# ScalarE's W1/W3 work in an attention and FFN block: scaling and rounding by halves, squares in step 11, sums by twos, and V's bound one group later

## The chip, the cores and the metric

One core of a Trainium2 chip runs the whole kernel in one launch. The metric is the device time in microseconds. Three runs of the kernel before gave 975.13, 976.01 and 978.0 us; the median is 976.01 us.

## What is computed

```python
xn = layernorm(x)                         # x: 2 x 1024 x 512
q, k, v = xn @ Wq.T, xn @ Wk.T, xn @ Wv.T # 16 heads of 32
scores = q @ k.T / sqrt(32), causal
s = (softmax(scores) @ v) @ Wo.T
hidden = silu(xn @ W1.T) * (xn @ W3.T)    # 2048 wide
hidden = fwht(hidden)                     # Walsh-Hadamard, / sqrt(2048)
g = silu(hidden @ W2.T)
return x + s * g
```

Inputs and output are fp32.

## The kernel before

Two batches of 1024 rows are worked off one after the other, each in three stages: project (Q, K, V and the first heads' maxima), heads (16 heads of attention, and beside head j the FFN's hidden tile j of W1 and W3), and tail (output projection, the down projection, the gate). Exactness is kept by splitting each operand into a rounded high part and a low rest, so most products are three matmuls. The transform is applied to W2 instead of hidden: GpSimd does butterfly steps on four slabs of W2 (slab_step), TensorE the last 128-point part in batch 0's tail.

**Heads.** A head has twelve steps (NS = 12, steps 0 to 11), each a tile of transposed scores: widths 512, 384, 256, 128, then 512 five times, 384, 256, 128. The five engines run program orders written out by hand, indexed by the global step g = 12 j + s. In step s of head j:

- TensorE makes scores(g) (line 1455), which needs exp(g - 2) to be done since there are two score banks; a share of the 48 FFN matmuls of tile j (FFN_SHARE, line 1494); maxima of later heads (line 1439); the context of four steps at a time, in steps 7, 10 and 3 of the next head; and in step 7 the transpose of the next head's maxima (line 1445). FFN groups alternate between two banks. The second bank is free again when VectorE's hide (line 1190) is done; it runs in steps 4 and 11.
- ScalarE does exp(g) (line 819), then probs_hi(g - 1) (line 829, the rounding to fp16), in some steps tanh, copies of the context, and the W1/W3 work below.
- GpSimd masks diagonal tiles (line 656, steps 0 to 3 and 8 to 11), combines the context, forms the low parts of W1/W3 in four pieces after exps 3 to 6 of the head (line 664), and in batch 0 does butterfly steps: in heads 0 to 2 some of slab 2, in heads 4 to 11 two of slab 3, after the masks of steps 10 and 11.
- VectorE does maxima (line 1148), probs_lo(g - 1) (line 1161, subtracts p_hi), gate, hide, and m_lo.
- SP's queue issues, per head, the three loads of the stack for head j + 2, in batch 0 the scan load of tile j + 4, the load of W1/W3 tile j + 2 (waits for GpSimd's last low piece), and the two stores of the maxima. After head 3's it stores slab 2 and loads slab 3.

**W1/W3.** A tile is 128 x 2 x 512 in fp32 (W1 part, W3 part). It is scaled by a power of two per tile (scale_w13, line 811, in place, two 128x512 instructions) and rounded to fp16 (w13_high, line 864, one 128x1024 instruction). The power comes from the mean square of the tile over all rows: in batch 0 a second load of each tile (scan) is squared and summed along its rows by ScalarE (w13_squares, line 854), TensorE adds over partitions (sum_of_squares, line 1421) and VectorE makes the scales of a group of tiles with five small operations (scale_of_w13). Tile 0 is its own group, tiles 1 to 3 are the second, then come groups of SCAN_GROUP tiles. There is one buffer for scans from tile 4 on, so the scan load of tile t waits for the squares of tile t - 1.

**V's bound.** In batch 0's project stage TensorE multiplies ones with the absolute values of Wv after projection group BOUND_AFTER (bound_of_v, line 1408). It waits for x16_lo of tile 6 (and so for all before it) because its bank M held the transposes. VectorE turns the result into a scale, scales Wv in place (line 1012) after the groups in WV_AT, ScalarE rounds (line 736) one group later, VectorE subtracts (line 1016) two groups later. The first V group (group 16) needs all of it. SP's scans of tiles 2 and 3 load into wv_raw and wait for the same.

Of the kernel before, what the change touches and what calls it, by code (L numbers as in the profile page):

```python
# [29 lines left out]
P = 128  # L30
# [37 lines left out]
SQUARES_AT, W13_AT = 5, 2  # L68
WO_AT = [1, 2, 7, 9]
WV_ABS_AFTER = {5: (0, 1), 6: (2, 3)}  # L70
BOUND_AFTER = 8
WV_AT = {9: (0, 1), 10: (2, 3)}
# [14 lines left out]
SCAN_FIRST, SCAN_GROUP = 4, 3  # L87
# [22 lines left out]
def build(nc, x, wq, wk, wv, wo, w1w3, w2, hadamard, out):  # L110
# [6 lines left out]
    with ctx:  # L117
# [15 lines left out]
        with ExitStack() as r:  # L133
# [9 lines left out]
        w13_ssq = sb("w13_ssq", [P, JT], F32)  # L143
        w13_pow, w13_scale, w13_half, w13_unscale = (
            sb(n, [P, JT], F32) for n in ("w13_pow", "w13_scale", "w13_half", "w13_unscale"))
# [17 lines left out]
        with ExitStack() as r:  # L163
# [14 lines left out]
            sb("room_before_x", [P, 2 * D - 2 * NT - 3 * P - W], F32, r)  # L178
# [145 lines left out]
        SUM_PLAN = {scan_groups[n][-1] - SCAN_FIRST: n for n in range(1, len(scan_groups))}  # L324
# [280 lines left out]
        def _(pool):  # L605
# [53 lines left out]
            def w13_low(n, piece):  # L659

                pool.wait_ge(w13_hi_done, n + 1)
                at = (slice(None), piece // 2, slice(piece % 2 * (D // 2), (piece % 2 + 1) * (D // 2)))
                pool.wait_ge(w13_scaled, 2 * n + piece // 2 + 1)
                pool.tensor_tensor(w13_lo[n % 2][at], w13[at], w13_hi[n % 2][at], ALU.subtract  # L664
                                   ).then_inc(w13_lo_done, 1)
# [63 lines left out]
        def _(act):  # L729
# [26 lines left out]
            def project(b):  # L756
# [34 lines left out]
                for t in range(NT):  # L791
# [4 lines left out]
                    if t == 1:  # L796
                        scale_w13(b * NH)
                        w13_high(b * NH)
# [6 lines left out]
            def scale_w13(n):  # L805
# [4 lines left out]
                for m in range(2):  # L810
                    act.activation(w13[:, m, :], w13[:, m, :], ACT.Copy, scale=w13_scale[:, n % NH:n % NH + 1]
                                   ).then_inc(w13_scaled, 1)
# [44 lines left out]
            def w13_high(n):  # L857

                if n < NH:
                    act.wait_ge(w13_scale_step, scale_steps(n))  # L860
                act.wait_ge(w13_in, (n + 1) * 16)
                after(act, ffn_ps, (n - 1) * GROUPS)
                act.wait_ge(w13_scaled, 2 * n + 2)
                act.activation(w13_hi[n % 2][:], w13[:], ACT.Copy).then_inc(w13_hi_done, 1)  # L864
# [8 lines left out]
            def heads(b):  # L873
# [5 lines left out]
                for g in range(SLOTS + DRAIN):  # L879
# [14 lines left out]
                    if s == W13_AT - 1 and j + 1 < NH:  # L894
                        scale_w13(n0 + j + 1)
                    if s == W13_AT and j + 1 < NH:
                        w13_high(n0 + j + 1)
# [745 lines left out]
```

## Time and profile before

| | |
|---|---|
| median of the runs | 976.01 us |
| the profiled execution | 981.31 us |
| its span | 979.6 us |
| mean granted TensorE clock | 0.994 |
| PE busy | 947.8 us (97%) |
| DVE busy | 732.3 us (75%) |
| ACT busy | 619.0 us (63%) |
| POOL busy | 337.8 us (34%) |

PE is TensorE (PEld its weight loads), DVE VectorE, ACT ScalarE, POOL GpSimd, SP SyncE (SPq its DMA queue). Busy time is the union of an engine's instructions; matmuls overlap one another, so a busy PE is not PE at its peak. "Idle before, releaser" is the time in which an engine had nothing to run, and what ended it. The heads of batch 0 begin at about 88 us; those of batch 1 end at about 861 us. The granted clock of a stretch is given as a share of 2.4 GHz.

### The profile page before, as it was taken

Reading aid. Unit: us, or ns where it says so; the run is one execution under the profiler, and the core shown is the slowest. Engines: PE = TensorE matmul, PEld = TensorE weight load, DVE = VectorE, ACT = ScalarE, POOL = GpSimd, SP = SyncE. Lnnn points to the kernel's source line nnn. Section 1 sums busy time; section 2 is a strip of 40 time slices with the busy share of each in tenths; the row PEclk is TensorE's granted clock in tenths of the full one; section 3 lists DMA queues with packets and bytes.
Section 4 is the critical chain, followed back from the end, with each engine's and each line's share of the span. In section 5 each row is a group of like instructions: output and inputs, shape, how many; then the busy total and the mean of one; then the engine's idle time right before and its main releaser. Section 6 shows DMA issues by size and latency. Waiting matters only on the chain. (4 is left out here: it accounts for less than half of the span.)

```text
span 979.6 us, 18781 instructions
## 1 busy us (share of the span) xinstructions
PE 947.8 (97%) x6404; PEld 652.1 (67%) x6404; DVE 732.3 (75%) x1487; ACT 619.0 (63%) x1284; POOL 337.8 (34%) x588
## 2 busy tenths in 40 slices
PE   8899999799999999999999999999999999999997
PEld 7786555455555565788888875565666656578886
DVE  7877998688998988655655568988989898833343
ACT  4445878588888787643344338888788887833221
POOL 1995663355555444000000013534444344410000
PEclk9999999899999999999999999999999999999999
DMA  9695335523433412892116722232322322171111
GB/s 289 235 307 171 87 101 152 128 77 98 129 78 98 110 44 74 280 361 71 44 54 236 230 73 65 77 87 56 99 66 77 88 69 63 45 320 67 43 43 44
DMA packets 57919, 118.46 MB, mean 121 GB/s; under 512 B 5600, under 2 KB 22624, under 8 KB 57312
## 3 DMA queue, kind: packets, MB, share of 16 engines
q1 hardware_dynamic: 57824, 117.27, 39.5%
q8 instruction: 51, 0.84, 0.4%
q14 instruction: 44, 0.36, 0.1%
HBM read 83.43 MB, written 33.55 MB: 119 GB/s over the span
## 5 line engine op out<-in xcount | busy, mean ns | idle before, releaser
L1161 DVE TENSOR_TENSOR p_lo<-stages,p_hi 128x512 f16<-128x512 f32 (+2 forms) x288 | 204.6, 716 | 56.7 <-ACT p_hi L829 52.5
L1494 PE MATMUL f<-x_hi,w_hi 128*128 128x512 f16 x512 | 195.7, 382 | 9.0 <-DVE hidden L1190 9.0
L1494 PE MATMUL f<-x_hi,w_lo 128*128 128x512 f16 x512 | 196.9, 385 | 0.0
L1494 PE MATMUL f<-x_lo,w_hi 128*128 128x512 f16 x512 | 195.6, 382 | 0.0
L819 ACT ACTIVATE stages<-s 128x512 f32<-128x512 f32 (+2 forms) x288 | 150.7, 523 | 53.9 <-PE s L1455 50.4
L829 ACT ACTIVATE p_hi<-stages 128x512 f16<-128x512 f32 (+2 forms) x288 | 159.6, 554 | 27.9 <-POOL stages L656 12.4
L1455 PE MATMUL s<-qk_st 98*128 98x512 f32 (+2 forms) x384 | 166.2, 434 | 6.3 <-ACT stages L819 6.3
L1148 DVE CUSTOM_DVE_ANT_0 m<-m,causal 128x1024 f32<-128x1024 f32 (+3 forms) x128 | 131.1, 1024 | 2.4 <-PE m L1439 2.3
L656 POOL TENSOR_SCALAR_AFFINE_SELECT stages<-stages 128x128 f32<-128x128 f32 x192 | 59.8, 319 | 188.8 <-ACT stages L819 188.7
L664 POOL TENSOR_TENSOR w_lo<-w,w_hi 128x256 f16<-128x256 f32 x128 | 96.0, 777 | 65.4 <-ACT w_hi L864 53.7
L1228 DVE TENSOR_TENSOR h_lo<-hidden,h_hi 128x1024 fp32r<-128x1024 f32 x32 | 39.2, 1225 | 84.6 <-ACT h_hi L914 84.6
L914 ACT ACTIVATE h_hi<-hidden 128x1024 fp32r<-128x1024 f32 x32 | 34.0, 1061 | 105.4 <-PE f L1305 105.4
L1303 PE MATMUL f<-g_hi,h_hi 128*128 128x512 f32 x256 | 99.7, 389 | 0.0
L1304 PE MATMUL f<-g_lo,h_hi 128*128 128x512 f32 x256 | 99.6, 389 | 0.0
L1305 PE MATMUL f<-g_hi,h_lo 128*128 128x512 f32 x256 | 99.6, 389 | 0.0
L1494 PEld LDWEIGHTS f<-x_hi,w_lo 128*128 128x128 f16 x512 | 50.2, 98 | 63.7 <-issue 32.8
L1439 PE MATMUL m<-qk_st 96*128 96x512 f32 (+3 forms) x256 | 91.8, 440 | 0.6 <-DVE mx L1148 0.6
L1455 PEld LDWEIGHTS s<-qk_st 98*128 98x128 f32 x384 | 73.2, 191 | 22.4 <-ACT stages L819 7.6
L1494 PEld LDWEIGHTS f<-x_lo,w_hi 128*128 128x128 f16 x512 | 50.5, 99 | 53.3 <-issue 8.7
L1473 PE MATMUL o<-vparts,p_hi 128*128 128x65 f16 x1152 | 83.7, 194 | 1.0 <-DVE p_lo L1161 1.0
L1494 PEld LDWEIGHTS f<-x_hi,w_hi 128*128 128x128 f16 x512 | 50.9, 99 | 50.3 <-issue 18.0
L1475 PE MATMUL o<-vparts,p_lo 128*128 128x65 f16 x1152 | 83.1, 193 | 0.0
(200 smaller groups left out, 1960.3 us busy)
## 6 DMA issues: line engine op xcount, KB each, us to landing
qk_st<-qk_parts SPq DMA_DIRECT2D x96, 256.0 KB, 4.3
w<-w1w SPq DMA_DIRECT2D x32, 512.0 KB, 3.6
qk_parts<-qk_hi SPq DMA_DIRECT2D x32, 256.0 KB, 3.4
qk_parts<-qk_lo SPq DMA_DIRECT2D x32, 256.0 KB, 4.3
scan<-w1w SPq DMA_DIRECT2D x12, 512.0 KB, 5.8
wht_in<-w SPq DMA_DIRECT2D x4, 1024.0 KB, 11.0
w_butterflied<-wht_in SPq DMA_DIRECT2D x4, 1024.0 KB, 5.9
w_transformed<-g_hi SPq DMA_DIRECT2D x8, 512.0 KB, 3.1
```

Of the source, the lines that this page charges most:

```text
L664: pool.tensor_tensor(w13_lo[n % 2][at], w13[at], w13_hi[n % 2][at], ALU.subtract).then_inc(w13_lo_done, 1)
L819: act.activation(expd[q % NE][:, 0:end - need], SB[q % 2][:, 0, need - start:end - start], ACT.Exp).then_inc(exp_done, 1)
L829: act.activation(p_hi[s][:], expd[q % NE][:, 0:end - need], ACT.Copy).then_inc(p_hi_done, 1)
L1148: dve.tensor_tensor_reduce(out=bank, in0=bank, in1=causal[:, S - width:S], scale=1.0, scalar=LOWEST, op0=ALU.add, op1=ALU.max, accum_out=m ...
L1161: dve.tensor_tensor(p_lo[s][:], expd[q % NE][:, 0:end - need], p_hi[s][:], ALU.subtract).then_inc(p_lo_done, 1)
L1303: pe.matmul(o, a_hi, b_hi, start=first, stop=False)
L1304: pe.matmul(o, a_hi, b_lo, start=False, stop=False)
L1305: return pe.matmul(o, a_lo, b_hi, start=False, stop=last)
L1439: mm = pe.matmul(bank[:, at:end], q[0:STACK, t * P:(t + 1) * P], k[0:STACK, at:end], start=True, stop=True)
L1455: pe.matmul(SB[q % 2][:, 0, 0:end - start], k_st[n % NH % 3][0:STACK + 2, k * P:(k + 1) * P], q_st[n % NH % 3][0:STACK + 2, start:end], st ...
L1473: pe.matmul(o, p_hi[s][:, at:at + P], v, start=k == 0 and t == c * TPC, stop=False, skip_group_check=True)
L1494: mm = pe.matmul(F[m][:, 0, :], w, v, start=k == 0, stop=k == GMM - 1)
```

## The change

- The squares of tiles 4 to 15 move from step 5 of heads 0 to 11 to step 11.
- Scale and round work by halves: the W1 half is scaled in step 1, rounded in step 2; the W3 half is scaled in step 2, rounded in step 3. In the project stage both halves are scaled and then both rounded. GpSimd's low pieces wait for their own half.
- Groups of tiles from tile 4 on have two tiles (six groups where there were four), and a group's sum is taken in step 7 of the head after the one that squared its last tile.
- V's bound and everything on Wv come one group later (in both batches for the scaling and the splits).
- w13_ssq and w13_pow (16 values a partition each) lie in a region that is reused later.

```diff
--- before.py
+++ after.py
@@ -65,11 +65,12 @@
 LOWEST = -3e38
 CTX_AT = [7, 10, 15]
 COPY_AT = [8, 4]
-SQUARES_AT, W13_AT = 5, 2
+SQUARES_AT = 11
+SCALE_AT, HIGH_AT = [1, 2], [2, 3]
 WO_AT = [1, 2, 7, 9]
 WV_ABS_AFTER = {5: (0, 1), 6: (2, 3)}
-BOUND_AFTER = 8
-WV_AT = {9: (0, 1), 10: (2, 3)}
+BOUND_AFTER = 9
+WV_AT = {10: (0, 1), 11: (2, 3)}
 MAX_BEFORE = {1: [0], 2: [1, 2], 3: [3, 4], 4: [5, 6], 5: [7]}
 MT_BEFORE = 7
 NB = 4
@@ -84,7 +85,7 @@
 SCAN_AFTER = {10: (1,), 13: (2, 3)}
 SQUARES_AFTER = {8: (0,), 13: (1,)}
 SQUARES_OF_V = {4: (2,), 5: (3,)}
-SCAN_FIRST, SCAN_GROUP = 4, 3
+SCAN_FIRST, SCAN_GROUP = 4, 2
 SPLIT_WK_AFTER, ROOT_AFTER = 1, 2
 BUSY_FIRST, BUSY_LAST = 42, 6
 STATS_AT = [(0, 1), (1, 1)]
@@ -140,9 +141,7 @@
         stats = sb("stats", [P, NT, 6], F32)
         mv = sb("mv", [P, NT, 2], F32)
         var, std, rstd, tmp = (sb(n, [P, NT], F32) for n in ("var", "std", "rstd", "tmp"))
-        w13_ssq = sb("w13_ssq", [P, JT], F32)
-        w13_pow, w13_scale, w13_half, w13_unscale = (
-            sb(n, [P, JT], F32) for n in ("w13_pow", "w13_scale", "w13_half", "w13_unscale"))
+        w13_scale, w13_half, w13_unscale = (sb(n, [P, JT], F32) for n in ("w13_scale", "w13_half", "w13_unscale"))
 
 
         with ExitStack() as r:
@@ -175,7 +174,8 @@
             m_lo = sb("m_lo", [NT, P], F32R, r)
             ones_r = sb("ones_r", [P, P], F32R, r)
             qk_lo3 = sb("qk_lo3", [P, W], F32R, r)
-            sb("room_before_x", [P, 2 * D - 2 * NT - 3 * P - W], F32, r)
+            w13_ssq, w13_pow = (sb(n, [P, JT], F32, r) for n in ("w13_ssq", "w13_pow"))
+            sb("room_before_x", [P, 2 * D - 2 * NT - 3 * P - W - 2 * JT], F32, r)
             x16_hi = sb("x16_hi", [P, KT, S], F16, r)
             x16_lo = sb("x16_lo", [P, KT, S], F16, r)
             vparts = sb("vparts", [P, NT, NH, VC], F16, r)
@@ -321,7 +321,7 @@
             return X[:, 0, W - len(scan_groups[n]):W]
 
         scan_groups = [range(1), range(1, SCAN_FIRST)] + [range(t, t + SCAN_GROUP) for t in range(SCAN_FIRST, NH, SCAN_GROUP)]
-        SUM_PLAN = {scan_groups[n][-1] - SCAN_FIRST: n for n in range(1, len(scan_groups))}
+        SUM_PLAN = {-1: 1, **{scan_groups[n][-1] - SCAN_FIRST + 1: n for n in range(2, len(scan_groups))}}
 
         def scan_tile(t):
 
@@ -658,7 +658,7 @@
 
             def w13_low(n, piece):
 
-                pool.wait_ge(w13_hi_done, n + 1)
+                pool.wait_ge(w13_hi_done, 2 * n + piece // 2 + 1)
                 at = (slice(None), piece // 2, slice(piece % 2 * (D // 2), (piece % 2 + 1) * (D // 2)))
                 pool.wait_ge(w13_scaled, 2 * n + piece // 2 + 1)
                 pool.tensor_tensor(w13_lo[n % 2][at], w13[at], w13_hi[n % 2][at], ALU.subtract
@@ -794,22 +794,23 @@
                     act.activation(vparts[:, t, :, 0:DH], group_bank(g).rearrange("p (h d) -> p h d", h=NH),
                                    ACT.Copy).then_inc(proj_hi_done, 1)
                     if t == 1:
-                        scale_w13(b * NH)
-                        w13_high(b * NH)
+                        for m in range(2):
+                            scale_w13(b * NH, m)
+                        for m in range(2):
+                            w13_high(b * NH, m)
                     if b == 0:
                         for tile in SQUARES_OF_V.get(t, ()):
                             w13_squares(tile)
                     if t == MT_BEFORE - 1:
                         maxima_hi(b * NH)
 
-            def scale_w13(n):
+            def scale_w13(n, m):
 
                 act.wait_ge(w13_in, (n + 1) * 16)
                 if n < NH:
                     act.wait_ge(w13_scale_step, scale_steps(n))
-                for m in range(2):
-                    act.activation(w13[:, m, :], w13[:, m, :], ACT.Copy, scale=w13_scale[:, n % NH:n % NH + 1]
-                                   ).then_inc(w13_scaled, 1)
+                act.activation(w13[:, m, :], w13[:, m, :], ACT.Copy, scale=w13_scale[:, n % NH:n % NH + 1]
+                               ).then_inc(w13_scaled, 1)
 
             def exp(q):
                 c, k = STEPS[q % NS]
@@ -854,14 +855,11 @@
                 act.activation(scan_tile(n) if n else w13_hi[0][:], scan_tile(n), ACT.Square,
                                accum_out=w13_ssq[:, n:n + 1]).then_inc(w13_sum, 1)
 
-            def w13_high(n):
-
-                if n < NH:
-                    act.wait_ge(w13_scale_step, scale_steps(n))
-                act.wait_ge(w13_in, (n + 1) * 16)
+            def w13_high(n, m):
+
                 after(act, ffn_ps, (n - 1) * GROUPS)
-                act.wait_ge(w13_scaled, 2 * n + 2)
-                act.activation(w13_hi[n % 2][:], w13[:], ACT.Copy).then_inc(w13_hi_done, 1)
+                act.wait_ge(w13_scaled, 2 * n + m + 1)
+                act.activation(w13_hi[n % 2][:, m, :], w13[:, m, :], ACT.Copy).then_inc(w13_hi_done, 1)
 
             def maxima_hi(n):
                 act.wait_ge(mt_ps, n + 1)
@@ -891,10 +889,11 @@
                             tanh(n0 + jf, c)
                     if b == 0 and s == SQUARES_AT and j + SCAN_FIRST < NH:
                         w13_squares(j + SCAN_FIRST)
-                    if s == W13_AT - 1 and j + 1 < NH:
-                        scale_w13(n0 + j + 1)
-                    if s == W13_AT and j + 1 < NH:
-                        w13_high(n0 + j + 1)
+                    for m in range(2):
+                        if s == SCALE_AT[m] and j + 1 < NH:
+                            scale_w13(n0 + j + 1, m)
+                        if s == HIGH_AT[m] and j + 1 < NH:
+                            w13_high(n0 + j + 1, m)
                     if g - 1 in MT_PLAN:
                         maxima_hi(n0 + MT_PLAN[g - 1])
                     if 0 <= g - SLOTS - CT_AT - 1 < 2:
```

## Rows read from the trace of the kernel before

**Rows 1.** Waits of PE: us in total, times, longest us.

```profile
PE f L1494 <- DVE hidden L1190: 9.0, 10, 1.0
PE s L1455 <- ACT stages L819: 6.3, 1, 6.3
...
PE m L1408 <- DVE x_lo L1059: 1.3, 1, 1.3
```

**Rows 2.** Line 1445, five stretches: ns min/median/max, first to last start (us).

```profile
L1445 PE MATMUL xs<-ident,mx x4: 272/273/275, 101.5 to 157.7; 128*8 128x128 f32 x4
...
L1445 PE MATMUL xs<-ident,mx x2: 272/273/274, 157.7 to 175.2; 128*8 128x128 f32 x2
...
L1445 PE MATMUL xs<-ident,mx x2: 273/274/274, 175.2 to 201.5; 128*8 128x128 f32 x2
...
L1445 PE MATMUL xs<-ident,mx x8: 272/272/276, 201.5 to 332.4; 128*8 128x128 f32 x8
...
L1445 PE MATMUL xs<-ident,mx x15: 272/273/274, 597.6 to 840.0; 128*8 128x128 f32 x15
```

**Rows 3.** Head 4: ACT timeline; window 181:186, its last three PEclk, DMA, GB/s.

```profile
180.24 1.06 ACT L854 ACTIVATE scan<-scan 128x1024 f32<-128x1024 f32 x1 [7.33 <-DMA scan<-w1w]
...
181.00:186.00 5.00, 4.08 (x10) 1.89 (x11) 2.75 (x4) 5.00 (x13) 1.39 (x3) 0.50 0.32 105
```

**Rows 4.** SP's queue, 166 to 172: issues, then (last number) us to landing.

```profile
166.47 4.64 SPq L377 DMA_DIRECT2D qk_st<-qk_parts  x3
171.16 0.42 SPq L497 DMA_DIRECT2D scan<-w1w  x1
...
qk_st<-qk_parts SPq DMA_DIRECT2D x2, 256.0 KB, 6.9
scan<-w1w SPq DMA_DIRECT2D x1, 512.0 KB, 9.1
```

**Rows 5.** ACT in head 5: the squares and the exp behind them.

```profile
199.12 1.05 ACT L854 ACTIVATE scan<-scan 128x1024 f32<-128x1024 f32 x1
...
200.16 0.59 ACT L819 ACTIVATE stages<-s 128x512 f32<-128x512 f32 x1
```

**Rows 6.** A head of batch 1: ACT and DVE, steps 11 to 0.

```profile
672.39 0.41 ACT L829 ACTIVATE p_hi<-stages 128x256 f16<-128x256 f32 x1
673.69 0.60 ACT L819 ACTIVATE stages<-s 128x512 f32<-128x512 f32 x1 [0.89 <-PE s L1455]
...
672.83 0.42 DVE L1161 TENSOR_TENSOR p_lo<-stages,p_hi 128x256 f16<-128x256 f32 x1 [0.37 <-ACT p_hi L829]
```

**Rows 7.** Head 6, end: timeline of POOL, DVE and PE.

```profile
227.13 1.27 POOL L642 TENSOR_TENSOR wht_in<-wht_in 128x512 f32<-128x512 f32 x1
...
227.14 1.55 DVE L1161 TENSOR_TENSOR p_lo<-stages,p_hi 128x256 f16<-128x256 f32 x1
228.61 0.73 DVE L1190 SCALAR_TENSOR_TENSOR hidden<-hidden,w_unscale,f 128x512 f32<-128x512 f32 x1
...
229.40 0.39 PE L1494 MATMUL f<-x_hi,w_hi 128*128 128x512 f16 x1 [1.02 <-DVE hidden L1190]
```

**Rows 8.** Head 4, end: timeline of DVE and POOL.

```profile
190.15 0.42 DVE L1161 TENSOR_TENSOR p_lo<-stages,p_hi 128x256 f16<-128x256 f32 x1 [0.21 <-ACT p_hi L829]
...
190.24 1.47 POOL L642 TENSOR_TENSOR wht_in<-wht_in 128x512 f32<-128x512 f32 x1
```

**Rows 9.** Groups by line: xcount | busy us, mean ns | idle before.

```profile
L1421 PE MATMUL xs<-w_ssq,ones_r 128*128 128x3 f32 (+1 forms) x12 | 1.7, 210 | 0.0
```

**Rows 10.** ACT's groups by line and form, the same columns.

```profile
L829 ACT ACTIVATE p_hi<-stages 128x512 f16<-128x512 f32 x160 | 99.5, 622 | 0.2
...
L864 ACT ACTIVATE w_hi<-w 128x1024 f16<-128x1024 f32 x32 | 33.8, 1057 | 0.2
```

**Rows 11.** Project stage of batch 0: timeline of DVE and PE.

```profile
58.39 2.94 DVE L1016 TENSOR_TENSOR w_lo<-wv_raw,w_hi 128x512 fp32r<-128x512 f32 x2
...
63.03 0.39 PE L1303 MATMUL f<-w_hi,xt_hi 128*128 128x512 f32 x1
```

## The prediction

> **What bounds the kernel.** I read the waits of TensorE first, then the spacing of heads, then the places where the spacing breaks. The waits name three things [rows 1]: ten waits of up to 1.0 us on VectorE's line 1190, one of 6.3 us on an exp of ScalarE, one of 1.3 us on VectorE's line 1059. They add up to less than what is lost, because matmuls overlap and a short stop hides in them. So I take one TensorE instruction that comes once a head, the transpose of the maxima in step 7, and measure from one to the next. In batch 1 it is (840.0 - 597.6) / 14 = 17.31 us a head [rows 2]. In batch 0 the three heads up to 157.7 and the seven from 201.5 to 332.4 take 18.7 us each, head 3 to 4 takes 17.5, head 4 to 5 takes 26.3. The work on TensorE is the same in both batches except for the small sums of squares. From 101.5 to 332.4 batch 0 spends 230.9 us on twelve heads; at batch 1's pace it would be 207.8. **23.1 us** is what batch 0 loses in that stretch, and it is where the squares of W1/W3 are.
>
> The 26.3 us head is one event. ScalarE sits for 7.33 us in front of the squares of tile 8, waiting for the tile [rows 3]; all later exps stand behind it in program order, TensorE runs out of scores to make and stops for 6.3 us, and afterwards its granted clock is 0.50 (the 1.2 GHz level) over 181 to 186. Clock and stop together are 26.3 - 17.3 = 9.0 us. The tile was late because the queue of SP had store_slab(2) and load_slab(3), 1 MB each, ahead of it: the next stack's loads took 4.64 us to issue, the scan was issued at 171.16 and landed 9.1 us later, at 180.2 [rows 4].
>
> **The squares, moved to step 11.** In step 5 ScalarE is in its densest stretch: the squares start at 199.12 and the exp behind them at 200.16, so each costs 1.04 us of ScalarE there and everything up to step 10 is 1.04 us late [rows 5]. In step 11 ScalarE has room: in a head of batch 1 it waits 0.89 us for TensorE right behind p_hi of step 10 [rows 6]. 1.04 us put there (they overlap p_hi's end by 0.1) delays one exp by about 0.1 us, and that exp has two slots of TensorE's work before its score bank is wanted, so I cost the squares at nothing in their new place; without that gap it would be 1.04 us a head. The late tile: step 7's transpose of head 4 is at 175.2, step 11's squares come 5.9 us later (ScalarE's p_hi of step 10 starts at 672.39, 5.6 after the transpose of that head at 666.8, and lasts 0.4) [rows 2, 6], at 181.1; the tile lands at 180.2. It just fits, with 0.9 us to spare, and if it slips it meets the idle gap first. What is late next there is stack 6, whose last part is issued at about 170.2 and lands 6.9 later, at 177.1 [rows 4]; TensorE's first maxima of head 6 want it some 2 us after 175.2, so at most some tenths are lost. SP's queue is the other thing that the move touches: the scan of the next tile waits for the squares, which end about when SP has issued the stack; the W1/W3 load behind it waits anyway for GpSimd's last low piece, which comes after step 6's exp of that head. Nothing.
>
> How much of the other 1.4 us a head comes back? Two things are mixed in it. In head 6 line 1190 starts at 228.61 and TensorE gets to go at 229.40 after 1.02 us of idling [rows 7]. Ahead of line 1190 on VectorE stands the p_lo of step 10, and it takes 1.55 us where the same form takes 0.42 in batch 1 [rows 6, 7]: it ends 0.3 us after a butterfly step of GpSimd that started 10 ns before it (227.13 + 1.27). So 1.1 us of lateness is GpSimd's, and step 9's p_lo has a butterfly step beside it too. Heads 0 to 2 and 4 to 11 have these butterfly steps; head 3 has none, pays 17.5 and not 18.7. But head 4, whose ScalarE and VectorE were ahead of the slow TensorE, has them too and loses nothing by them: p_lo of step 10 starts at 190.15, the second butterfly step only at 190.24 [rows 8]. With ScalarE 1.04 us earlier, the masks and with them the butterfly steps start some 0.9 us earlier against TensorE, and TensorE itself is ready some 0.4 us earlier (1.4 lost less 1.0 seen as idle). Then it goes one of two ways: p_lo of step 10 starts first, as in head 4, and line 1190 is in time: 0. Or GpSimd starts first, and 1.0 (seen) + 0.15 (the part of a stop that hides behind the matmul before it) - 0.9 + 0.4 = 0.6 us a head is left. In head 6 the two starts are 10 ns apart [rows 7], so I can't tell which and take the middle, **0.3 us in each of 11 heads, 3.3 us** (0 to 6.6). The squares' term is 23.1 - 3.3 = 19.8 us.
>
> The rule behind this is in the Trainium skill, SBUF — State Buffer, section SBUF: two separate sides: VectorE with two SBUF inputs and GpSimd take a shared port pair as an exclusive lock, whoever starts first, for the whole instruction. The rows agree, and read strictly the rule gives either end, 0 or 6.6 us, not my middle.
>
> **Sums every second head.** Two more sums: twelve records of line 1421 with 1.7 us are six sums, each under 0.3 us of TensorE [rows 9], so 2 x 0.3 = 0.6 us at most; VectorE's five small operations for a sum are in the mean of 18.7 us of batch 0 already, where every third head has them, and VectorE isn't TensorE's releaser there. I take **0.5 us lost** together. The sums are asked for in step 7 and their last squares ended with step 11 of the head before, so TensorE doesn't wait for them.
>
> **Scaling and rounding by halves.** A 128x1024 rounding lasts 1057 ns, a 128x512 one 622 [rows 10], and the next instruction starts about 0.1 us before the end of the last. So two halves cost 2 x 0.52 against 0.96, **0.09 us of ScalarE a head**, 2.8 us over 32 tiles. In batch 1 ScalarE has a gap of 0.89 us a head between steps 11 and 0 alone [rows 6], so TensorE sees nothing; if that cover were gone it would be 2.8 us. The exps of steps 2 and 3 come 0.4 to 0.6 us earlier; nobody waits for them, since heads without squares run at 17.31 with TensorE busy throughout. GpSimd's low pieces wait for step 3's exp and step 4's copy, behind the second half as well. Cost 0, range -0.5 to 2.8. The Trainium skill, ScalarE: Activation LUTs, section What ACT_TABLE_LOAD costs, speaks against halves: 186 ns + 0.833 ns an element, 93 ns of it overlapped, so a split costs 93 ns. The rows give the same, and by that rule all 32 would be 3 us if ScalarE set the pace.
>
> **V's bound one group later.** TensorE idles 1.3 us ahead of it, for VectorE's x16 of tiles 6 and 7 [rows 1]. A group (2.7 us) later these are done: 1.3 us back. But the scale, and all eight operations on V's weights, follow one group later on VectorE, and in batch 0 they take 1.4 us each beside the butterflies (two end at 61.33; V's first group starts at 63.03) [rows 11]. VectorE is back to back from group 9 on; I get its last split at 62.0 us, 0.7 later than now (a group of 2.7 us later, less TensorE's 1.3 and the room of 0.7 between groups), and TensorE there at 63.03 - 1.3 = 61.7. So 1.3 - 0.3 = **1.0 us gained** (0 to 1.3). In batch 1 nothing waits.
>
> **Sum.** 19.8 - 0.5 + 1.0 - 0 = 20.3 us. The profiled execution, 981.3 us (span 979.6), would come to 961.0. The median of the runs is 976.0, 5.3 below it; the stop and the spacing belong to the program, so I take the same off: **955.7 us**. Moving two small tensors of 64 bytes a partition changes no instruction.
>
> **Rivals.**
> (a) GpSimd always starts first, in all 11 heads: 11 x 0.6 = 6.6 us are left in place of 3.3, 959. For it: head 6 [rows 7]. Against it: head 4 [rows 8]. The rule of the Trainium skill's page SBUF — State Buffer named above gives just this if GpSimd wins each time.
> (b) Line 1190 is late because of the butterflies alone and the squares' shift does nothing for it. Then only the hidden 0.4 us a head, head 3's 0.2 and head 4's 8 us come back: 4.0 + 0.2 + 8 + 0.5 = 12.7, 963.3. Against it: head 4 again.
> (c) The stop at head 4 doesn't go but shrinks, because scan or stack 6 lands later than in this trace: 2 to 5 us more, 958 to 961.
> (d) The other side: ScalarE's stretch from step 11 to step 1 of the next head turns critical. The squares hold exps, p_hi and tanh, TensorE waits for the gate, and the whole squares are paid, plus the wait for a tile that is now asked for only after step 11. Against today's loss of 23 us it must cost over 1.9 us in each of 12 heads, that is, the tile must land more than 2 us behind step 11; it is issued some 17 us before and lands in 6 to 9. At 2.2 us a head it would be 979.
> (e) The move does nothing: tiles too late in step 11 also. That is (c) or (d).
>
> **Chances.** The forecast with its middle (952 to 958.9) 0.52; (a) 0.2; (b) 0.13; (c) 0.1; (d) 0.03; the rest is between. Best case: 23.1 - 0.3 + 1.3, 951.9. Down to 951 and up to 964, (a), (b) and (c) are inside. 0.3% (about 3 us) is what a measurement can tell here. Faster by more 0.95, within 0.02, slower 0.03.
>
> **What would show it.** Right: no wait on the scan tile, no 6.3 us stop, no stretch at 0.50 in batch 0's heads; transposes 17.3 to 17.9 us apart in heads 0 to 11; line 1190's waits gone or at 0.6; the wait ahead of line 1408 gone, perhaps a shorter one at V's first group. Wrong: spacing still at 18 us or more, a new wait on stack loads near head 4, or batch 1's spacing off 17.31, which would mean that the halves cost.

## The result and the profile after

The changed kernel takes **964.16 us** (median of four runs, 963.12 to 969.42) against 975.65 us for the kernel before (four runs, 975.13 to 978.0): a ratio of 0.9888, 95% interval 0.9849 to 0.9928. The forecast was 955.7 us with a range of 951 to 964, so the direction was right and the time 8.5 us off, just outside the range. The profiled execution took 964.6 us, 0.4 above its median.

The head of the page after, with the engines' busy times (share of the span, instructions):

```profile
span 962.9 us, 18863 instructions
PE 943.5 (98%) x6408; PEld 651.6 (68%) x6408; DVE 735.5 (76%) x1497; ACT 624.4 (65%) x1316; POOL 335.6 (35%) x588
```

TensorE is still the bound. Its waits after (us in total, times, longest), to be put beside [rows 1]:

```profile
PE f L1493 <- DVE hidden L1189: 5.7, 10, 1.0
...
PE s L1454 <- DMA qk_st<-m_lo: 0.4, 1, 0.4
```

The 6.3 us wait on ScalarE at head 4 and the wait ahead of V's bound are gone. The hide waits went from 9.0 to 5.7 us, which is far from gone, and a small wait on a store of the maxima's rows is new in the list. The same transpose as in [rows 2], after (ns min/median/max, first to last start):

```profile
L1444 PE MATMUL xs<-ident,mx x4: 272/272/273, 100.5 to 155.1; 128*8 128x128 f32 x4
...
L1444 PE MATMUL xs<-ident,mx x2: 273/273/273, 155.1 to 172.5; 128*8 128x128 f32 x2
...
L1444 PE MATMUL xs<-ident,mx x2: 272/272/273, 172.5 to 190.6; 128*8 128x128 f32 x2
...
L1444 PE MATMUL xs<-ident,mx x8: 272/272/275, 190.6 to 316.6; 128*8 128x128 f32 x8
...
L1444 PE MATMUL xs<-ident,mx x15: 272/272/273, 579.5 to 823.2; 128*8 128x128 f32 x15
```

The seven spacings from 190.6 on take 126.0 us, 18.0 each where they took 18.7. Head 3 to 4, which has no butterfly step, takes 17.4; head 4 to 5 takes 18.1 instead of 26.3. Batch 1 has become **slower**: 243.7 / 14 = 17.41 us a head, where [rows 2] give 242.4 / 14 = 17.31.

The span fell by 979.6 - 962.9 = 16.7 us. The transposes cut it into pieces. The first transpose comes at 84.0 instead of 84.9, and 16.5 us instead of 16.6 pass to the second (1.0 us gained). The twelve heads take 216.1 instead of 230.9 (14.8 gained). From 316.6 to batch 1's 579.5 are 262.9 us, from 332.4 to 597.6 they were 265.2 (2.3 gained). Batch 1's fourteen spacings lose 1.3, and behind them nothing changes (139.7 us and 139.6). 1.0 + 14.8 + 2.3 - 1.3 is 16.8, the rest is rounding. But the medians differ by 11.5 us only, so some 5 us of the 16.7 are peculiar to the one execution of the kernel before that was profiled; the experiments show which.

### The profile page after: what moved, and what is told of

The parts are those of the page before. It is cut to its first block and busy times, and to the rows that moved or that the text cites. A ratio compares the mean times of both kernels' runs of the same rounds, so it can differ in the third digit from the quotient of the medians.

```text
span 962.9 us, 18863 instructions
## 1 busy us (share of the span) xinstructions
PE 943.5 (98%) x6408; PEld 651.6 (68%) x6408; DVE 735.5 (76%) x1497; ACT 624.4 (65%) x1316; POOL 335.6 (35%) x588
## 5 line engine op out<-in xcount | busy, mean ns | idle before, releaser
L1160 DVE TENSOR_TENSOR p_lo<-stages,p_hi 128x512 f16<-128x512 f32 (+2 forms) x288 | 211.6, 743 | 33.0 <-ACT p_hi L830 32.7
L1147 DVE CUSTOM_DVE_ANT_0 m<-m,causal 128x1024 f32<-128x1024 f32 (+3 forms) x128 | 131.0, 1023 | 2.3 <-PE m L1438 2.3
L656 POOL TENSOR_SCALAR_AFFINE_SELECT stages<-stages 128x128 f32<-128x128 f32 x192 | 62.2, 330 | 168.7 <-ACT stages L820 168.0
L1472 PEld LDWEIGHTS o<-vparts,p_hi 128*128 128x128 f16 x1152 | 74.1, 97 | 12.8 <-DVE p_lo L1160 1.2
```

The lines of the kernel that those rows point to most:

```text
L1147: dve.tensor_tensor_reduce(out=bank, in0=bank, in1=causal[:, S - width:S], scale=1.0, scalar=LOWEST, op0=ALU.add, op1=ALU.max, accum_out=m ...
L1160: dve.tensor_tensor(p_lo[s][:], expd[q % NE][:, 0:end - need], p_hi[s][:], ALU.subtract).then_inc(p_lo_done, 1)
L1472: pe.matmul(o, p_hi[s][:, at:at + P], v, start=k == 0 and t == c * TPC, stop=False, skip_group_check=True)
```

## Experiments

Twelve kernels were run in three sessions, each with the kernel before beside them (975.53, 975.95 and 976.6 us). Ratios are against those. "Spacing" is the time between two step-7 transposes.

### Is it the halves, the butterflies, or the squares?

**The changed kernel with whole tiles again** (two scalings in step 1, one 128x1024 rounding in step 2, as before):

```diff
-                    for m in range(2):
-                        if s == SCALE_AT[m] and j + 1 < NH:
+                    if s == 1 and j + 1 < NH:
+                        for m in range(2):
                             scale_w13(n0 + j + 1, m)
-                        if s == HIGH_AT[m] and j + 1 < NH:
-                            w13_high(n0 + j + 1, m)
+                    if s == 2 and j + 1 < NH:
+                        w13_high(n0 + j + 1)
```

> The changed kernel with scaling and rounding of a tile whole again (both scalings in step 1, one 128x1024 rounding in step 2). Theory H (the halves cost 0.1 us of ScalarE a head and ScalarE sets the pace of steps 1 to 4): batch 1's spacing falls from 17.41 back to 17.31 us, batch 0's too by 0.1, about 3 us faster than the changed kernel, 961 us. Rival (the 0.1 us a head comes from the shifted addresses or the later work on Wv): spacing stays 17.41, 964 us.

Measured: 961.75 us (961.21 to 965.72), ratio 0.9861 (0.984 to 0.9881), 2.4 us under the changed kernel. Batch 1's transposes in this kernel:

```profile
L1443 PE MATMUL xs<-ident,mx x14: 272/273/273, 598.6 to 824.4; 128*8 128x128 f32 x14
```

225.8 / 13 = 17.37 us; two spacings among them are longer (17.81, which holds a wait of 0.23 us for the store of a maxima row, and 17.63), the eleven others are back at 17.31. The heads with butterflies stay at 17.9 to 18.1. Over all profiles the median spacing of batch 1 is 17.31 us in the eight profiles of kernels that round whole tiles and have batch 1 otherwise unchanged, and 17.40 to 17.41 in the five with halves. So the halves cost 0.10 us in each head that nothing else holds up: batch 1, and in batch 0 heads 3, 12 and 13 (17.41, 17.56, 17.40 with halves; 17.32 in the combined kernel below, 17.47, 17.31 here). In the heads with butterflies they cost nothing, and the first spacing of a batch is 0.15 us shorter with them (16.23 against 16.38 in batch 1). That is about 1.4 us in all; the 2.4 between the medians is within the spread of the runs.

**The changed kernel with one butterfly step of a head moved** from behind step 11's mask to behind step 2's (heads 0 to 2 and 5 to 11), so that none stands beside the p_lo ahead of the hide:

```diff
                         mask(n * NS + s)
+                        if s == 2:
+                            if n < LAST_SLAB_AT - 1:
+                                late_steps(1)
+                            if b == 0 and 0 < j - LAST_SLAB_AT < 8:
+                                of = j - LAST_SLAB_AT
+                                slab_step(D // P - 1, of // 2, of % 2, 0)
...
-                        if n < LAST_SLAB_AT - 1 and s >= NS - 2:
+                        if n < LAST_SLAB_AT - 1 and s == NS - 2:
                             late_steps(1)
                         of = j - LAST_SLAB_AT
-                        if b == 0 and 0 <= of < 8 and s >= NS - 2:
+                        if b == 0 and of == 0 and s >= NS - 2:
                             slab_step(D // P - 1, of // 2, of % 2, s - NS + 2)
+                        if b == 0 and 0 < of < 8 and s == NS - 2:
+                            slab_step(D // P - 1, of // 2, of % 2, 1)
```

> The changed kernel with the butterfly step that followed step 11's mask moved behind step 2's mask of the same head (heads 0 to 2 and 5 to 11); that of step 10 stays. Theory B (the 0.5 to 0.6 us a head left in batch 0 is step 11's butterfly holding the p_lo of step 10, and with it line 1189): waits on line 1189 vanish, spacing of those heads 17.4 to 17.5 us, 5 to 6 us faster, about 958.5 us. Rival (the rest is due to the squares in step 11, on ScalarE): spacing stays near 18.0, 964 us.

Measured: 961.72 us (961.0 to 962.36), 0.9854 (0.9833 to 0.9876), 2.4 us under the changed kernel, where 5.7 were expected. The end of head 6 shows how it works. In the changed kernel (timelines of POOL, DVE and PE: start, us, instruction, idle before; L656 is GpSimd's mask, L642 its butterfly step, L1147 a maximum of VectorE):

```profile
214.57 0.45 POOL L656 TENSOR_SCALAR_AFFINE_SELECT expd<-expd 128x128 f32<-128x128 f32 x1
214.99 1.28 POOL L642 TENSOR_TENSOR wht_in<-wht_in 128x512 f32<-128x512 f32 x1
...
214.12 0.74 DVE L1160 TENSOR_TENSOR p_lo<-stages,p_hi 128x384 f16<-128x384 f32 x1
214.79 0.28 DVE L1147 CUSTOM_DVE_ANT_0 xs<-xs,causal 128x128 f32<-128x128 f32 x1
...
215.00 1.55 DVE L1160 TENSOR_TENSOR p_lo<-stages,p_hi 128x256 f16<-128x256 f32 x1
...
216.47 0.73 DVE L1189 SCALAR_TENSOR_TENSOR hidden<-hidden,w_unscale,f 128x512 f32<-128x512 f32 x1
...
217.26 0.39 PE L1493 MATMUL f<-x_hi,w_hi 128*128 128x512 f16 x1 [0.53 <-DVE hidden L1189]
```

and with the step moved (DVE), followed by its PE wait on the hide and its transposes of heads 6 to 11:

```profile
213.66 0.41 DVE L1168 TENSOR_TENSOR p_lo<-stages,p_hi 128x256 f16<-128x256 f32 x1
214.00 0.73 DVE L1197 SCALAR_TENSOR_TENSOR hidden<-hidden,w_unscale,f 128x512 f32<-128x512 f32 x1
```

```profile
PE f L1501 <- DVE hidden L1197: 0.5, 1, 0.5
```

```profile
L1452 PE MATMUL xs<-ident,mx x6: 273/273/273, 207.3 to 294.7; 128*8 128x128 f32 x6
```

GpSimd again starts 10 ns ahead of p_lo, as in [rows 7], and p_lo again takes 1.55 us; alone it takes 0.41. The wait of the next FFN group is 0.53 where it was 1.02: the squares' move halved it and the butterfly holds the rest. Without the butterfly the ten waits of 5.7 us become one of 0.5, that of head 4, which keeps its step, and the spacing is 87.4 / 5 = 17.5. The twelve heads take 210.8 us, 5.3 less. Not all arrives. The spacing from the first transpose to the second grew from 16.45 to 17.10, and in the three other kernels with the moved step, which round whole tiles, it is 17.70, where whole tiles without it have 16.60: the step costs 0.6 to 1.1 us where it goes in the first head, which was not forecast. And in this execution TensorE waited 1.6 us for h_lo, VectorE's low part of hidden, in batch 0's tail, where the changed kernel's profile has 0.4; the profile of the kernel before has this wait with 1.6 and the next one of the same kernel not, so it varies from execution to execution.

**The changed kernel with the squares back in step 5:**

```diff
-SQUARES_AT = 11
+SQUARES_AT = 5
```

> The changed kernel with the squares back in step 5 and nothing else undone. It measures the term of the squares by itself. Theory: the 6.3 us stop at head 4 is back, and the spacing of heads 0 to 11 is 18.7 to 18.8: 7 x 0.7 + 1.0 + 6.3, some 13 to 15 us slower than the changed kernel, 977 to 979 us. Rival (the halves and the sums by twos gave part of the gain): less, 970 us.

Measured: 977.14 us (975.08 to 980.87), 1.0013 (0.9999 to 1.0026), 13.0 us over the changed kernel. The whole gain of the change, within the spread, is this line. Its transposes of the last eight heads, and ScalarE's squares in head 4:

```profile
L1444 PE MATMUL xs<-ident,mx x8: 272/273/275, 196.7 to 328.0; 128*8 128x128 f32 x8
```

```profile
175.73 1.06 ACT L855 ACTIVATE scan<-scan 128x1024 f32<-128x1024 f32 x1 [2.64 <-DMA scan<-w1w]
```

18.75 us a head, 18.7 without one spacing of 19.30 that holds a store wait of 1.3 us, what [rows 2] show. But the wait for the tile is 2.6 us, not the 7.33 of [rows 3], and TensorE's stop behind it is 1.4 us, not the 6.3 that were expected to come back.

**The kernel before with the halves alone** (all of the halves' edits, squares still in step 5, nothing else):

> The kernel before with only the scaling and rounding by halves. Theory: 0.1 us a head in batch 1 and in batch 0's heads without a butterfly (3, 12 to 15): spacing 17.41, 1.5 to 3 us slower than before, 977.5 us. Rival (halves help the dense stretch with the squares in step 5): batch 0's spacing below 18.7, up to 2 us faster.

Measured: 977.26 us (975.53 to 980.47), 1.0014 (0.9997 to 1.003). The times alone can't tell this from nothing; the trace can:

```profile
L1448 PE MATMUL xs<-ident,mx x15: 273/273/274, 590.8 to 834.5; 128*8 128x128 f32 x15
```

243.7 / 14 = 17.41, the same as in the changed kernel, to 10 ns.

**The kernel before with that butterfly step moved**, squares in step 5:

> The kernel before with step 11's butterfly behind step 2's mask (heads 0 to 2, 5 to 11), squares in step 5. It splits the 1.4 us a head. Theory (the squares' lag alone costs what head 3 shows, 0.2 to 0.35 us a head; the rest needs the butterfly and the lag together): spacing 17.5 to 17.8 us in those heads, 8 to 11 us faster than before, 966 us, with the stop at head 4 still there. Rival (the squares in the dense stretch cost the most): spacing stays above 18.2, at most 4 us faster.

Measured: 969.48 us (967.18 to 970.89), 0.9925 (0.9901 to 0.9949), 7.1 us under the kernel before, where 8 to 11 were expected.

```profile
L1453 PE MATMUL xs<-ident,mx x7: 273/273/275, 214.0 to 320.8; 128*8 128x128 f32 x7
```

106.8 / 6 = 17.80; five of the six spacings are 17.56 to 17.82, and the one of 18.58 holds a wait of 0.7 us for a maxima store. Take the heads without a sum of squares: with the squares in step 5 and no butterfly beside p_lo they take 17.56 to 17.62, 0.3 us over 17.31; with the butterfly and the squares in step 11 (heads 5 to 11 of the changed kernel with whole tiles) 17.87 to 17.94, 0.6 over it; with both, in the kernel before, 18.7, 1.4 over it. The two add up to less than what both cost together: each is partly hidden as long as the other is away.

### What was peculiar to the profiled execution

**The kernel before, unchanged, profiled once more:**

> The kernel before, unchanged, for a second profile. Theory (the profile before the change caught a long stop: its execution took 981.3 us against a median of 975.6): the head 4 to 5 spacing is 21 to 24 us in place of 26.3, with a granted clock of 1.00 behind the stop or nearly, execution 974 to 978 us; the spacings of the other heads are the same 18.7 and 17.3 us. Rival (the 5 us lie elsewhere, spread over the run): the spacing is 26 us again.

Measured: 977.47 us (ten runs, 973.72 to 979.92), 1.0006 (0.9986 to 1.0027); the execution profiled this time took 975.64 us with a span of 973.9, against 981.3 and 979.6. Head 4 in it (ACT; transposes of heads 3 to 5; PE busy and the rest of a window, last three PEclk, DMA, GB/s):

```profile
176.87 1.06 ACT L854 ACTIVATE scan<-scan 128x1024 f32<-128x1024 f32 x1 [3.28 <-DMA scan<-w1w]
```

```profile
L1445 PE MATMUL xs<-ident,mx x3: 273/273/273, 156.9 to 197.9; 128*8 128x128 f32 x3
```

```profile
180.00:185.00 5.00, 5.00 (x48) 3.19 (x46) 4.37 (x9) 3.79 (x10) 2.75 (x6) 0.75 0.36 109
```

The tile landed at 176.87, 3.4 us earlier than in [rows 3], though the kernel is the same: SP issued it at 169.04 instead of 171.16, and it landed 7.8 us later instead of 9.1. TensorE stopped 2.2 us instead of 6.3, its granted clock was 0.75 in the stretch behind and not 0.50, and heads 3 and 4 took 40.9 us together, a store wait of 1.2 us in head 3 included, where they took 17.5 + 26.3 = 43.8. The expectation of a clock near 1.00 behind the stop did not come true. In the six further profiles of kernels with the squares in step 5 and the loads in their order (this one, the halves alone, the bound alone, the groups of two, the moved butterfly, and the changed kernel with its squares back), heads 3 and 4 together took 40.5 to 41.7 us, and TensorE's stop was 1.4 to 3.9 us; 43.8 and 6.3 were seen once. A second such piece lies at the head of batch 0's tail, in the first profile of the kernel before:

```profile
395.00:400.00 5.00, 4.86 (x14) 3.83 (x15) 3.08 (x5) 2.37 (x5) 0.00 (x0) 0.66 0.53 190
```

and after, at the same point of the program:

```profile
379.00:384.00 5.00, 5.00 (x26) 4.07 (x25) 3.36 (x7) 3.62 (x8) 0.00 (x0) 1.00 0.74 267
```

A clock of 0.66 for 5 us is worth 5 x 0.34 = 1.7 us, and the wait for h_lo of 1.6 us stands there too. From the last transpose of batch 0 to the first of batch 1 that execution took 214.2 us; the six other profiles of the kernel before and its variants have 210.8 to 211.0, the changed kernel 211.7 and its variants 211.0 to 213.0. So 2.1 to 3.3 us at head 4 and some 3.3 in the tail were of that one execution, about the 5 us by which profile and median disagree.

**The kernel before with slab 3's 1 MB load behind head 4's scan** on SP's queue:

```diff
                             scan_w13(j + SCAN_FIRST)
+                        if b == 0 and j == LAST_SLAB_AT:
+                            load_slab(3)
...
-                        load_slab(3)
```

> The kernel before with the load of slab 3 put behind head 4's scan load on SP's queue; squares stay in step 5. It takes away the late tile alone. Theory: ScalarE no longer waits for the scan at head 4, its spacing is 18.7, and the time is 2 to 4 us shorter (972 us), more against an execution with a long stop. Rival (the tile is late for lack of bandwidth, whatever the order, or the stop moves to GpSimd, which then waits for slab 3): no gain.

Measured: 972.77 us (970.08 to 975.7), 0.997 (0.9954 to 0.9985), 3.2 us under the kernel before. ScalarE no longer waits for the tile, and head 4 to 5 is 18.81 us:

```profile
L1446 PE MATMUL xs<-ident,mx x3: 273/273/273, 157.6 to 194.9; 128*8 128x128 f32 x3
```

Heads 3 and 4 take 37.3 us together. So the stop did come from the queue's order, and it is worth 3.2 us by the medians and 3.2 to 4.4 by those two heads (a store wait of 0.75 us is in the 37.3). In the first profile it was 26.3 - 18.8 = 7.5; the 9.0 that I read there had the 1.4 us of squares and butterflies in it and was of one execution.

### V's bound and the sums

**The changed kernel with the bound one group earlier again**, and **the kernel before with the bound one group later**:

```diff
-BOUND_AFTER = 9
-WV_AT = {10: (0, 1), 11: (2, 3)}
+BOUND_AFTER = 8
+WV_AT = {9: (0, 1), 10: (2, 3)}
```

> The changed kernel with V's bound and the work on Wv one group earlier again. Theory: the first transpose of the maxima comes 0.9 us later (85.0 in place of 84.0), all else the same, 965 us. Rival (the later work on Wv gives nothing, or the batch 1 spacing depends on it): no difference, or spacing 17.31.

> The kernel before with only V's bound and the work on Wv one group later. Theory: the wait ahead of line 1408 is gone, a new one of some 0.3 us ahead of V's first group, the first transpose of the maxima 0.9 us earlier, 0.9 us faster, 975.0 us; within the spread. Rival: no change.

Measured: 965.05 us (964.64 to 966.47), 0.989 (0.9871 to 0.9909), 0.9 over the changed kernel, which the spread of the four runs of each doesn't set apart, and its first transpose at 85.0 instead of 84.0. The other: 976.08 us (973.73 to 980.3), 0.9993 (0.9974 to 1.0012), first transpose at 84.97, no gain to be seen. The waits of PE, first in the one, then in the other:

```profile
PE m L1407 <- DVE x_lo L1058: 1.4, 1, 1.4
```

```profile
PE f L1303 <- DVE w_lo L1016: 1.2, 1, 1.2
```

In the profile of the kernel before with the later bound the wait only moves to V's first group, nearly as long as it was. In the changed kernel's profile that wait is away; there VectorE's first scaling of Wv took 681 ns against 1174 here. The seven profiles with the later bound fall the same way: five with 680 to 683 ns and no such wait, two (this one, and the changed kernel with its squares back, 1657 ns) with one of 1.2 and 1.0 us. That the scaling is the cause is what the durations suggest; no run set it apart. The stage also varies: the first transpose came at 84.15 to 85.01 us in seven profiles with the earlier bound (mean 84.7), unchanged kernels at 84.92 and 84.24 among them, and at 83.51 to 84.97 in seven with the later one (mean 84.1). The bound is worth 0.6 us by the means, with a spread as large. Part of the spread is a stop of TensorE of 1.0 us at about 38 us, with no releaser in the profile, which eleven of the fourteen profiles have.

**The kernel before with groups of two tiles:**

```diff
-SCAN_FIRST, SCAN_GROUP = 4, 3
+SCAN_FIRST, SCAN_GROUP = 4, 2
```

with the plan of the sums from the change.

> The kernel before with only the sums of squares every second head (six groups in place of four), squares in step 5. Theory: two more sums, together at most 0.5 us, nothing that can be measured, 976 us. Rival (VectorE's small operations lengthen the heads that have a sum): 1 to 3 us slower.

Measured: 976.42 us (973.97 to 977.48), 0.9998 (0.9984 to 1.0012): nothing that the time shows. But the trace shows what a sum costs where nothing hides it. Head 12 has no butterfly and no squares; here it has a sum, in the kernel before it has none. Its transpose and the two behind it, here and in the kernel before:

```profile
330.03 0.27 PE L1445 MATMUL xs<-ident,mx 128*8 128x128 f32 x1
...
347.50 0.27 PE L1445 MATMUL xs<-ident,mx 128*8 128x128 f32 x1
...
364.80 0.27 PE L1445 MATMUL xs<-ident,mx 128*8 128x128 f32 x1
```

```profile
332.37 0.27 PE L1445 MATMUL xs<-ident,mx 128*8 128x128 f32 x1
...
349.67 0.27 PE L1445 MATMUL xs<-ident,mx 128*8 128x128 f32 x1
```

With the sum 17.47 us, without it 17.30. In the changed kernel heads 6 to 11 take 18.06 to 18.10 with a sum and 17.91 to 17.96 without one; in the changed kernel with the step moved 17.53 to 17.56 and 17.38 to 17.41. In the kernel before, the four heads with a sum are no longer than the others (18.6 to 18.7 us against 18.7 to 18.8): there the wait on the hide is 0.73 us instead of 1.0.

### Putting it together

**The changed kernel with whole tiles and the butterfly step moved** (the two edits shown above):

> The changed kernel with whole tiles for scaling and rounding and with step 11's butterfly behind step 2's mask. Theory: both gains add, all spacings near 17.31 to 17.5, 959 us. Rival (with the dense stretch whole again, the butterfly in step 2 collides with it): no better than either alone, 961.7 us.

Measured: **958.66 us** (958.15 to 959.58), 0.982 (0.9796 to 0.9843): 17.3 us under the kernel before and 5.5 under the changed one, better than both. Batch 1 is at 243.1 / 14 = 17.36, its last spacing of 18.04 included, the others at 17.31; heads 6 to 11 are at (311.7 - 206.9) / 6 = 17.5:

```profile
L1451 PE MATMUL xs<-ident,mx x7: 272/273/274, 206.9 to 311.7; 128*8 128x128 f32 x7
...
L1451 PE MATMUL xs<-ident,mx x15: 272/273/273, 574.3 to 817.4; 128*8 128x128 f32 x15
```

**The same, and in step 4 the context's copy behind p_hi on ScalarE and the denominators behind the hide on VectorE**, to shorten the chain that I suspected of setting 17.31:

```diff
-                    if s == COPY_AT[1] and j > 0:
-                        copy_o(n0 + j - 1, 1)
                     if g < SLOTS:
                         exp(n0 * NS + g)
                     if 1 <= g <= SLOTS:
                         probs_hi(n0 * NS + g - 1)
+                    if s == COPY_AT[1] and j > 0:
+                        copy_o(n0 + j - 1, 1)
...
-                    if s == COPY_AT[1] and j > 0:
-                        denominators(n0 + j - 1, 1)
...
                             hide(n0 + jf, c)
+                    if s == COPY_AT[1] and j > 0:
+                        denominators(n0 + j - 1, 1)
```

> The combined version a_best with, in step 4, ScalarE's copy of the context behind p_hi of step 3 and VectorE's denominators behind line 1189's hide. It takes 0.26 us out of the chain from step 1's exp to step 4's hide. Theory (this chain, ScalarE's dense stretch and then VectorE, sets the pace of 17.31 us): batch 1's spacing falls to 17.05 to 17.2 us and the whole by 3 to 7 us, 953 to 956. Rival (TensorE's own work is 17.3 us a head): spacing stays 17.31, 958.7 us.

Measured: 962.05 us (958.24 to 964.75), 0.9851 (0.9822 to 0.9881): not faster as a whole. But batch 1 fell below 17.31:

```profile
L1451 PE MATMUL xs<-ident,mx x13: 272/273/275, 593.9 to 800.9; 128*8 128x128 f32 x13
```

207.0 / 12 = 17.25, 0.06 less. Expected was more, and batch 0 gave nothing or lost. So 17.31 is not TensorE's own pace and the chain is part of what sets it, but something else stands right behind it, and what that is stays open, as does why the whole did not profit.

## Why the forecast was partly right

**The stop at head 4: right, its size misread.** The squares in step 11 find their tile. ScalarE and its exp in head 4, the issue of the scan on SP's queue, and its time to landing, after:

```profile
178.51 1.05 ACT L855 ACTIVATE scan<-scan 128x1024 f32<-128x1024 f32 x1
179.55 0.58 ACT L820 ACTIVATE stages<-s 128x512 f32<-128x512 f32 x1
```

```profile
166.01 0.42 SPq L497 DMA_DIRECT2D scan<-w1w  x1
...
scan<-w1w SPq DMA_DIRECT2D x1, 512.0 KB, 8.2
```

It lands at 174.2, 4.3 us before it is used, and the exp follows at once. The term of 9.0 us from [rows 3] was one draw. Heads 3 and 4 take 35.5 us after, against 43.8 in that profile and 40.5 to 41.7 in the others: 8.3 us once, 5.0 to 6.2 otherwise, the share of the squares and butterflies included. The slack of 0.9 us that I worked out went by the same late execution.

**The median: wrong.** The step "the stop and the spacing belong to the program, so I take the same off" failed. The execution was 5.3 us above its median because of the long stop and the slow clock in the tail, and the change removed one and did not meet the other again; so its profile was 0.4 above its median. 5.3 - 0.4 = 4.9 of the 8.5 us are this, the other 3.6 are 20.3 - 16.7. The mark was there: what made that execution an outlier had to lie somewhere in its trace, and I credited the same stop to the change in full and then subtracted it a second time.

**The butterflies: the middle of two ends was wrong.** I took 0.3 us a head between 0 (p_lo first) and 0.6 (GpSimd first). GpSimd started first in all eleven heads, and rival (a) was right in mechanism and price: heads without a sum take 17.91 us against 17.31, with halves and with whole tiles alike. That is 3.3 us. The Trainium skill, SBUF — State Buffer, section SBUF: two separate sides, describes the port pair as a lock that is held for the whole instruction; p_lo's 1.55 us behind a 1.28 us step and its 0.41 us without one agree. Starts 10 ns apart did not fall either way by chance: p_lo started 6 to 10 ns behind the butterfly step in every one of the eleven heads, and so it had in all ten heads but head 4 in the kernel before, where I had read one. The rows of head 6 above suggest why. VectorE's p_lo of step 9 ends, and behind it come a maximum of 0.28 us on VectorE and the mask on GpSimd, which shows 0.45 us where its length elsewhere is 0.29; both are over at about 215.0, and p_lo and the butterfly step follow. The two engines are set off by the same end, in every head. No run varied this. The price without the squares' lag and the lag without the butterflies were measured as well, and rival (b), that the squares' shift does nothing, fell with the kernel that puts them back (13.0 us).

**The halves: wrong, 1.3 us in batch 1 and 0.1 in head 3.** ScalarE's 0.09 us a head was right; that "TensorE sees nothing" was not. The cover that I named, the gap of 0.89 us between steps 11 and 0, lies before the halves, not between them and what waits for them. Steps 1 to 4 of ScalarE have no gap. A head of batch 1 in the kernel before (its transpose is at 684.16; ACT, then DVE, of step 4):

```profile
697.71 0.34 ACT L829 ACTIVATE p_hi<-expd 128x128 f16<-128x128 f32 x1
...
698.07 0.29 DVE L1161 TENSOR_TENSOR p_lo<-expd,p_hi 128x128 f16<-128x128 f32 x1
698.37 0.72 DVE L1190 SCALAR_TENSOR_TENSOR hidden<-hidden,w_unscale,f 128x512 f32<-128x512 f32 x1
```

and after (its transpose is at 683.97):

```profile
697.61 0.34 ACT L830 ACTIVATE p_hi<-expd 128x128 f16<-128x128 f32 x1
...
697.98 0.29 DVE L1160 TENSOR_TENSOR p_lo<-expd,p_hi 128x128 f16<-128x128 f32 x1 [0.52 <-ACT p_hi L830]
698.28 0.72 DVE L1189 SCALAR_TENSOR_TENSOR hidden<-hidden,w_unscale,f 128x512 f32<-128x512 f32 x1
```

From the transpose to p_hi are 13.55 us before and 13.64 after, to the hide 14.21 and 14.31: the 0.10 us goes straight through to step 4 and, by the spacing, around the loop. The second argument, that heads with "TensorE busy throughout" have no one waiting, failed too: TensorE counts as 100% busy at 17.31, at 17.41 and at 17.25. The sign that I had named for this, batch 1's spacing off 17.31, is what gave it away. The five profiles with halves and the eight without show it. The rule of the Trainium skill that I cited and then priced at nothing (ScalarE: Activation LUTs, section What ACT_TABLE_LOAD costs; an estimate of 93 ns for a split from its 186 ns an instruction, 93 of them overlapped) agrees with the 0.10 us of the spacing.

**V's bound: 1.0 us in the profiled pair, as forecast**, 0.6 by the means over many. The wait that I expected at V's first group was away in this profile and 1.2 us in the kernel before with the bound alone. **The squares in step 11: free, as forecast**: head 3, which has them and no butterfly, takes 17.41, the same as batch 1. **The sums: 0.15 us in each head that has one**, five of the twelve, 0.7 us where I took 0.5. I had priced only the two further ones, since the mean of 18.7 us held the others; but there they were hidden, and in the faster heads all of them show.

Together, against the sum of 20.3 us: -3.3 for the butterflies; -0.7 for head 1, which takes 18.64; -0.2 for the sums; -0.3 for head 3's halves (0.1) and for head 5 (0.15), which holds a store wait of 0.4 us; -1.3 for the halves in batch 1; +2.3 for the tail of the first profile. That is 16.8, and the spans differ by 16.7. Head 1 has a third butterfly step, behind GpSimd's low parts (118.49 us, 1.72 long), and beside it VectorE's two p_lo take 2.86 us where they take 1.77 a head later; it is long in the kernels with the moved step too (17.96 and 17.98 beside 17.4). I had priced it like the others. No run took this step away.

## What to carry to other kernels

Before a profiled execution that lies above the median is used for a sum, find what made it long; if the change removes that same event, its excess is counted once and not taken off again. A busy engine is no proof that it sets the pace: compare the spacing of an instruction that runs once an iteration, and follow a lengthened engine from the edit to the next wait of the loop, since only a gap between the two covers anything. Where two engines race for the SBUF ports with starts a few ns apart in a loop, read the race in every iteration of the trace and take the end that it shows, and not the middle. What a slower loop hides, as the sums here, has to be priced again when the loop gets faster.

## What had not been expected

- Stops of TensorE too short to be seen. The spacing went from 17.31 to 17.41 us with PE shown busy all along: a matmul shows 0.38 us and its successor starts 0.22 us later, so a stop of up to 0.16 us leaves no idle time.
- Issue and landing of a load behind 2 MB of others varied widely between executions of the same kernel: ScalarE waited 7.33 us for the tile of head 4 once and 3.28 the next time, TensorE stopped for 6.3 and 2.2 us, and its granted clock over 5 us behind the stop was 0.50 once and 0.75 the next time.
- Stores of a few KB were sometimes late. The scores of some head waited 0.2 to 1.4 us for the stores of the maxima's rows, in kernels that differ nowhere near; each of these shows as a single long spacing (18.58 instead of 17.6 in the kernel before with the moved step). They are not strewn at random: head 3 has one in five of the fourteen profiles, and in several the long spacings lie seven heads apart (heads 3 and 10 of batch 0, 1 and 8 of batch 1 in the second profile of the kernel before). Why is open.
- Moving the butterfly step gained 7.1 us with the squares in step 5, but 2.4 (halves) and 3.1 us (whole tiles) with the squares in step 11. Delays on two engines that meet in one wait have to be priced together.
